# The first and the last expert layer: from sorted tiles to every expert in blocks of 256 tokens

## Chip, cores and metric

One core of one Trainium2 chip. The metric is the device time of one execution in microseconds (us); of several executions the median is taken. The engines are called as in the profile: PE (TensorE, the matrix engine), PEld (its weight loads, which overlap its matmuls), DVE (VectorE), ACT (ScalarE), POOL (GpSimd), SP (SyncE, which only issues DMAs here).

## What is computed

The input is x of 16 sequences of 256 tokens, 128 wide, float32. Three layers act on it, each with a layer norm before it:

```python
x = x + 0.5 * ffn(layernorm(x))        # mixture of experts
x = x + attn(layernorm(x))             # two Mamba blocks, then a linear memory
x = x + 0.5 * ffn(layernorm(x))        # the same mixture again

def ffn(x):                            # E = 8 experts, hidden 512, top 2 of 8
    probs = softmax(x @ gate_w); vals, idx = top_k(probs, 2); vals /= sum(vals)
    combine = zeros(N, E) with vals at idx
    for e in range(E):
        out += combine[:, e:e+1] * (silu(x @ w1s[e]) @ w2s[e])
```

A token needs only its two experts; the other six have a weight of zero.

## The kernel before

The work goes in 8 groups of 2 sequences, that is 512 tokens or 4 tiles of 128 (GROUPS, SEQ, TILES). Each group passes through a first FFN, the mixer (four Mamba passes: two blocks by two sequences, then the memory), and a second FFN. The 16 FFNs of a group of 512 tokens are numbered by `first(g)` and `second(g)` in the order in which they run. The mixer of group g runs in four slots. In each slot the tables of ORDER write out by hand how every engine interleaves the scan's steps with those of an FFN of another group: while the mixer works on group g, the first FFN of g+1 and the second FFN of g-1 are done in pieces (`p` on PE, `F` on ACT, `sc` and `ga` on POOL). So fourteen FFNs lie inside the mixer slots. The first (group 0, number 0) has no mixer before it and is done in `start()`; the last (group 7, number 15) has none after it and is done in `finish()`.

An FFN sorts its tokens by expert. `ffn_stats` and `ffn_norm` (L977) normalise; POOL takes the root (`ffn_root`, L1287) and copies the residual (`ffn_keep`, L1301); `ffn_turn` (L407) transposes on PE, ACT copies (L723), `ffn_gate` (L413) makes the logits, `ffn_top` the two best experts, ACT their weights through a tanh (L728), `ffn_count` (L420 to L424) and `ffn_place` (L1008 to L1031) the place of each of the 1024 token copies in 15 tiles of 128 (NT) that hold one expert each. POOL scatters the copies by 8 indirect DMAs (L1308) to DRAM (`xs_d`, cleared to zero at the start), SP loads them in 5 chunks of 3 tiles (`chunk_in`), and the pieces follow: T transposes a chunk (L432), U multiplies a tile with the first weights of its expert (`ffn_up`, L441, four matmuls of 128x128), ACT applies silu (L747), D multiplies with the second (`ffn_down`, L450, four matmuls). The results go to DRAM by chunks (`chunk_out`), POOL gathers the two rows of each token by 8 indirect DMAs (L1317), and `ffn_sum` (L1048) adds them with their weights to the residual. A float32 matmul is two records in the trace. The first weights of a tile's expert are fetched by SP into a ring of four buffers (`expert_in`, `wst`, 256 KB each), the second ones (`w2s`, 2 MB) lie in SBUF.

`start()` of all engines: FFN 0; halfway through its pieces the routing of FFN 1, whose scatters run beside them; the mixer's constants on DVE (`mixer_weights`, L931 to L960); `ffn_sum` of FFN 0; then the norm, projections and first steps of the mixer of group 0. `finish()` of all engines: DVE closes the last scan (`gate_y`, L1151 to L1157, which waits until the eighth accumulating DMA, L1344, has landed), the memory of sequence 1 runs (`memory_1` to `memory_4`, L579 to L607, with `masked`, L1173, and `mixer_sum`, L1181), and only then the whole of FFN 15, beginning with the norm of all four tiles; the store of group 7 ends the program. Sequence 0 of group 7 has its mixer result in `xb` already in the last slot (`xb` in ORDER).

Of the kernel before, what the change touches and what calls it, by code (L numbers as in the profile page):

```python
# [82 lines left out]
MIDWAY = PIECES // 2  # L83
MIDWAY_LEFT = sum(1 for p in PIECE[:MIDWAY] if p[0] != "D" or p[1] % CH == CH - 1)

# [54 lines left out]
def moe_mamba_kernel(nc, x, pack, early, sel, w1, w2, out):  # L140
# [4 lines left out]
    with ctx:  # L145
# [57 lines left out]
        hit = sb("hit", [P, 2, TILES, E])  # L203
        xa = sb("xa", [P, TILES, D])
# [44 lines left out]
        empty = ys  # L249

# [8 lines left out]
        def sem(name):  # L259
# [19 lines left out]
            sem("f_hmm"), sem("f_hact"), sem("f_ymm"), sem("f_ys"), sem("f_yacc"))  # L279

# [42 lines left out]
        def _(sp):  # L323
# [4 lines left out]
            sp.wait_ge(s_clear, 1)  # L328
# [13 lines left out]
            def chunk_in(n, c):  # L342
                sp.wait_ge(s_scat, 16 * 2 * TILES * (n + 1))
                wait(sp, f_hmm, (n - 1) * ITEMS + RING_OF["T", c] + 1)
                sp.dma_start(xsort[:, c * CH:(c + 1) * CH, :], rows(xs_d[n % 2], c)).then_inc(s_xs[c], 16)

            def expert_in(n, i):
                k = n * NT + i
                sp.wait_ge(f_tile, n + 1)
                if k >= NW:  # L350
                    m, j = divmod(k - NW, NT)
                    sp.wait_ge(f_hmm, m * ITEMS + RING_OF["U", j] + 1)
                e = sp.value_load(eid[n % 2][0:1, i:i + 1], min_val=0, max_val=E - 1)
                sp.dma_start(wst[k % NW][:, :], w1[e]).then_inc(s_w[k % NW], 16)

            def chunk_out(n, c):
                wait(sp, s_gat, 16 * 2 * TILES * (n - 1))
                sp.wait_ge(f_ys, n * CHUNKS + c + 1)
                sp.dma_start(rows(ys_d[n % 2], c), ys[:, c * CH:(c + 1) * CH, :]).then_inc(s_ys[c], 16)
# [6 lines left out]
            def store(g):  # L366
                sp.wait_ge(f_yacc, second(g) + 1)
                sp.dma_start(ot[g], ob[:, :, :]).then_inc(s_store, 16)
# [3 lines left out]
            for n in range(2 * GROUPS):  # L372
# [8 lines left out]
                if n == 0:  # L381
                    for i, b in enumerate(sel_in):
                        sp.dma_start(b, sel[:, i * N_SEL:(i + 1) * N_SEL]).then_inc(s_sel, 16)
                    clear(xs_d[1])
# [8 lines left out]
            store(GROUPS - 1)  # L393
            sp.wait_ge(s_store, 16 * GROUPS)
# [3 lines left out]
        def _(pe):  # L398
# [3 lines left out]
            def ffn_turn(n, busy):  # L402
# [3 lines left out]
                for j in range(TILES):  # L406
# [3 lines left out]
            def ffn_gate(n):  # L410
                pe.wait_ge(f_xT, n + 1)
                for j in range(TILES):
                    last = mm(LG[:, j * E:(j + 1) * E], xT[:, j * P:(j + 1) * P], par("gate"), start=True, stop=True)  # L413
                last.then_inc(f_logits, 1)

            def ffn_count(n):
                pe.wait_ge(f_mask, n + 1)
# [9 lines left out]
            def ffn_sorted(n, c):  # L427
                r = RING_OF["T", c]
                pe.wait_ge(s_xs[c], 16 * (n + 1))
                wait(pe, f_hact, n * ITEMS + r - 1)  # L430
# [4 lines left out]
            def ffn_up(n, i):  # L435
                r, k, t = RING_OF["U", i], n * NT + i, i % CH * P
                pe.wait_ge(s_w[k % NW], 16 * (k // NW + 1))
                wait(pe, f_hact, n * ITEMS + max(r - 1, RING_OF["T", i // CH] + 1))
# [5 lines left out]
            def ffn_down(n, i):  # L444
                pe.wait_ge(f_hact, n * ITEMS + RING_OF["U", i] + 1)
                if i % CH == 0:
                    wait(pe, f_ys, n * CHUNKS + i // CH)
                e = pe.value_load(eid[n % 2][0:1, i:i + 1], min_val=0, max_val=E - 1)
# [9 lines left out]
            def turn(g, i):  # L458
# [4 lines left out]
                if i == 0 and 0 < g < GROUPS - 1:  # L463
                    pe.wait_ge(f_tile, first(g + 1) + 1)
                elif i == 2 and g > 0:
                    pe.wait_ge(f_tile, second(g - 1) + 1)
# [180 lines left out]
            def ffn_pieces(n, a, b):  # L647
                for x in range(a, b):
                    ffn_piece(n, x)

            def route(n):
                ffn_turn(n, None)
                ffn_gate(n)
                ffn_count(n)

            def start():
                route(first(0))
                pe.wait_ge(s_w2, 16)
                ffn_pieces(first(0), 0, MIDWAY)
                pe.wait_ge(f_tile, first(0) + 1)  # L660
                route(first(1))
                ffn_pieces(first(0), MIDWAY, PIECES)
                pe.wait_ge(s_set_dve, 1)
                pe.wait_ge(f_tile, first(1) + 1)
# [6 lines left out]
            def finish():  # L671
                tail = (GROUPS - 1, 1)
                memory_1(*tail, None)
                memory_2(*tail, None)
                memory_3(*tail)
                memory_4(*tail)
                route(second(GROUPS - 1))
                ffn_pieces(second(GROUPS - 1), 0, PIECES)
# [18 lines left out]
        def _(act):  # L697
# [27 lines left out]
            def ffn_gate(n):  # L725
                table(SILUS)
                act.wait_ge(f_gap, n + 1)
                do(th[:, :], gap[:, :], ACT.Tanh, scale=0.5).then_inc(f_th, 1)  # L728

            def ffn_leave(n, x):  # L730
                kind, k = LEAVES[x]
                if kind == "U":
                    table(SILUS)
                if kind == "Y":
                    act.wait_ge(f_ymm, n * NT + (k + 1) * CH)
# [747 lines left out]
```

## Time and profile before

| | us |
|---|---|
| three runs | 1793.55, 1782.19, 1767.53 |
| their median | 1782.19 |
| the profiled execution, its own time | 1785.28 |
| its span, first to last instruction | 1783.4 |
| mean granted TensorE clock in the span | 0.866 of full |

A clock of 1.00 is 2.4 GHz, one of 0.50 is 1.2 GHz; the records know only these two, and a number between is a mean over a stretch. Points of time in the text are us from the start of the span. In the timeline, a row is a run of equal instructions; its bracket gives the idle time of the engine ahead of them and what ended it.

### The profile page before, as it was taken

The numbers are of one execution on the slowest core, as the hardware profiler recorded it, in microseconds if no ns is written. First come the engines' busy times: TensorE is split into PE (matmuls) and PEld (weight loads), VectorE is DVE, ScalarE is ACT, GpSimd is POOL, SyncE is SP. The second block draws the span as 40 slices with busy tenths as digits, with TensorE's granted clock in tenths as the row PEclk, the third lists the DMA queues.
The fourth block names the chain that finished last, engine by engine and source line by source line (L and its number), as shares of the span: only waits on it lengthen the run. The fifth ranks groups of instructions, "written<-read, shape, count | busy, mean of one in ns | idle before, by whom it ended". The sixth has DMA issues, their size and how long they took to land. (4 is left out here: it accounts for less than half of the span.)

```text
span 1783.4 us, 29139 instructions
## 1 busy us (share of the span) xinstructions
PE 1313.4 (74%) x8528; PEld 1183.0 (66%) x8528; DVE 1366.4 (77%) x2144; ACT 1268.3 (71%) x2641; POOL 601.3 (34%) x639
## 2 busy tenths in 40 slices
PE   3738766887888788878888787878888786577434
PEld 2727655776877677767777676767777675567334
DVE  1227798889889888989888888989888979887400
ACT  1229775888789787878789787978787887487212
POOL 2221424144342526152433435163515322321311
PEclk9858967998989899998989899989999898589657
DMA  7415645666576767666666667676666664556323
GB/s 221 135 51 118 133 82 118 140 145 152 128 174 142 168 139 165 137 169 129 138 155 146 158 131 174 138 175 140 154 136 155 142 141 91 112 124 147 63 81 88
DMA packets 153383, 242.49 MB, mean 136 GB/s; under 512 B 14480, under 2 KB 87952, under 8 KB 153104
## 3 DMA queue, kind: packets, MB, share of 16 engines
q0 software_dynamic: 40448, 134.25, 38.9%
q1 hardware_dynamic: 112784, 106.38, 20.7%
q8 instruction: 76, 1.25, 0.3%
q14 instruction: 75, 0.61, 0.1%
HBM read 94.95 MB, written 28.18 MB: 69 GB/s over the span
## 5 line engine op out<-in xcount | busy, mean ns | idle before, releaser
L1344 POOL DMA_DIRECT2D acc<-G x224 | 204.7, 914 | 901.4 <-DVE G L1143 450.8
L809 ACT ACTIVATE dA<-delta,A 128x255 f32<-128x255 f32 x1024 | 425.7, 495 | 4.4 <-DVE hs L1124 3.4
L450 PE MATMUL b_out<-w2s,hT 128*128 x1920 | 282.4, 293 | 66.8 <-issue 44.0
L1130 DVE TENSOR_TENSOR_SCAN hs<-dA,b_r 128x512 f32<-128x512 f32 x256 | 298.9, 1203 | 25.8 <-PE b_r L545 15.2
L1143 DVE TENSOR_TENSOR G<-hs,b_r 128x1024 f32<-128x1024 f32 x224 | 272.3, 1216 | 58.3 <-PE b_r L556 51.3
L450 PEld LDWEIGHTS b_out<-w2s,hT 128*128 128x128 f32 x1920 | 249.6, 202 | 90.2 <-issue 89.0
L1124 DVE TENSOR_TENSOR_SCAN hs<-dA,dbu 128x1024 f32<-128x1024 f32 x128 | 292.6, 2286 | 13.8 <-ACT dA L809 7.3
L441 PE MATMUL b_h<-xsT,wst 128*128 128x128 f32 x1920 | 282.9, 295 | 10.0 <-ACT hT L747 7.3
L441 PEld LDWEIGHTS b_h<-xsT,wst 128*128 128x128 f32 x1920 | 262.3, 211 | 14.7 <-issue 12.2
L705 ACT ACT_TABLE_LOAD x180 | 230.9, 1283 | 4.0 <-PEq L1477 0.7
L825 ACT ACTIVATE scaled<-duT,dtT 128x256 f32<-128x256 f32 x512 | 217.0, 500 | 0.3
L747 ACT ACTIVATE hT<-b_h 128x512 f32<-128x512 f32 x240 | 139.8, 595 | 103.6 <-PE b_h L441 102.3
L545 PE MATMUL b_r<-prm,scaled 128*128 128x128 f32 x1024 | 174.4, 301 | 47.8 <-ACT scaled L825 26.7
L1308 POOL DMA_INDIRECT sorted<-xn,posi x128 | 154.3, 1206 | 105.1 <-DVE posi L1031 70.4
L545 PEld LDWEIGHTS b_r<-prm,scaled 128*128 128x128 f32 x1024 | 135.6, 157 | 61.8 <-issue 27.0
L556 PE MATMUL b_r<-bcr,selr 128*128 128x256 f32 x512 | 137.4, 353 | 48.4 <-DVE G L1143 39.0
L1317 POOL DMA_INDIRECT yk<-results,posi x128 | 139.0, 1086 | 93.5 <-DMA results<-ys 55.3
L1111 DVE TENSOR_TENSOR dbu<-du,b_r 128x1024 f32<-128x1024 f32 x128 | 155.2, 1212 | 12.0 <-PE b_r L538 11.9
L485 PE MATMUL b_w<-uT,inx 128*128 128x256 f32 x512 | 141.6, 414 | 1.4 <-ACT uT L754 1.4
L556 PEld LDWEIGHTS b_r<-bcr,selr 128*128 128x128 f32 x512 | 89.1, 210 | 64.1 <-DVE G L1143 49.4
L485 PEld LDWEIGHTS b_w<-uT,inx 128*128 128x128 f32 x512 | 96.6, 205 | 12.3 <-ACT uT L754 2.3
L432 PE MATMUL b_h<-prm,xsort 128*128 128x128 f32 x240 | 46.2, 307 | 67.2 <-DMA xsort<-sorted 41.6
(155 smaller groups left out, 1788.7 us busy)
## 6 DMA issues: line engine op xcount, KB each, us to landing
acc<-G POOLq DMA_DIRECT2D x224, 512.0 KB
wst<-w_dram SPq DMA_DIRECT2D x240, 256.0 KB, 3.0
xsort<-sorted SPq DMA_DIRECT2D x80, 192.0 KB, 5.6
results<-ys SPq DMA_DIRECT2D x80, 192.0 KB, 3.0
xin<-x_dram SPq DMA_DIRECT2D x8, 256.0 KB, 4.9
sorted<-xn,posi POOLq DMA_INDIRECT x128
yk<-results,posi POOLq DMA_INDIRECT x128
out_dram<-ob SPq DMA_DIRECT2D x8, 256.0 KB, 2.9
```

What stands on the lines that cost most here:

```text
L441: last = mm(H[r % 2][:, w], wst[k % NW][:, w], xsT[i // CH % 2][:, t:t + P], start=True, stop=True)
L450: last = mm(Y[:, i % CH * D:(i % CH + 1) * D], hT[i % NH][:, c, :], w2s[:, e, c, :], start=c == 0, stop=c == HC - 1)
L485: last = mm(o, inx[:, m, r, ch], uT[:, b, PAD - r:PAD - r + T], start=r == 0, stop=r == PAD)
L545: last = nc.tensor.transpose(R[u % 2][:, h * T + t * P:h * T + (t + 1) * P], scaled[k % 2][:, d, t, h * P:(h + 1) * P], ident)
L556: last = mm(C[:, d * T:(d + 1) * T], selr[:, SELECTED.index(DS + DP * j + d), :], bcr[b][:, :], start=True, stop=True)
L705: nc.scalar.preload_act_table_set(name)
L809: last = do(dA[j % 4][:, d, k, 1:], delta[b][:, k, 1:], ACT.Exp, scale=A[:, k, s:s + 1])
L825: last = do(scaled[n % 2][:, d, t, :], duT[b][:, t, :], ACT.Identity, scale=dtT[b][:, s:s + 1])
L1124: V.tensor_tensor_scan(flat(hs[j % 2]), flat(dA[j % 4]), flat(dbu[n % 2]), 0.0, ALU.mult, ALU.add)\
L1130: V.tensor_tensor_scan(hs[j % 2][:, d, :, :].rearrange("p h t -> p (h t)"), dA[j % 4][:, d, :, :].rearrange("p h t -> p (h t)"), R[u % 2][ ...
L1143: V.tensor_tensor(to[:, :, :, :], hs[j % 2][:, :, :, :], both(C).unsqueeze(2).broadcast_to([P, DP, HALVES, T]), ALU.mult).then_inc(q_G, 1)
L1344: Q.dma_start(acc[b][:, :, :, :].rearrange("p d h t -> p (d h t)"), G[j % NG][:, :, :, :].rearrange("p d h t -> p (d h t)"), accum_op=ALU. ...
```

## The change

FFN 0 and FFN 15 don't sort any more. Each is done as 16 blocks: one expert on 256 tokens (two tiles), all eight experts for all tokens. `STARTS` = 16 blocks make FFN 0, in the order expert by expert, both halves of the tokens for each; 16 more make FFN 15, all experts for sequence 0 and then all for sequence 1. FFN 15 is split in two numbers (LAST = 15 and 16), each with its own norm, routing and output store.

A block is `whole_up` (four matmuls with 256 moving columns, `w1` chunks as the stationary operand, the transposed tokens `xTd` moving, into the two banks H), two silus of 128x512 on ACT into `hTd`, `whole_down` (eight matmuls of 128x128 into the one bank OUT) and `whole_sum` on DVE: two scalar_tensor_tensor, which add OUT times the expert's combine weight (`comb`, zero where the expert isn't chosen) to the residual. PE issues `whole_up` of block x+1 ahead of `whole_down` of block x. The wait on `d_sum` keeps `whole_down` of block x behind `whole_sum` of block x-1.

In `start()` the norm, routing, count and placing of FFN 1 are put between these blocks (after blocks 0, 1, 4, 6, 9, 10), and `mixer_weights` after block 10 on DVE. The DMAs of SP are in a new order: the first weights of expert 0 in place of the first clearing of `xs_d`; the other first weights, the second group's x, the constants and then the two clearings behind. In `finish()` the first half (sequence 0) starts ahead of `gate_y`; the memory of sequence 1 lies between its blocks (after 16 to 19), and norm and routing of the second half after blocks 19 to 22. The fourteen sorted FFNs in the slots keep their work; their counters are shifted by one (`m = n - 1`).

```diff
@@ SP
-            clear(xs_d[0])
+            whole_in(0)
             sp.dma_start(w2s ...
-            sp.dma_start(win[:, 0:3 * DI], early[:, 0:3 * DI]).then_inc(s_early, 16)
-            sp.dma_start(taps, early[:, 3 * DI:]).then_inc(s_early, 16)
+            for b in range(2, 2 * NW, 2):
+                whole_in(b)
...
+            load_x(1)
+            sp.dma_start(win[:, 0:3 * DI], early[:, 0:3 * DI]).then_inc(s_early, 16)
+            sp.dma_start(taps, early[:, 3 * DI:]).then_inc(s_early, 16)
+            whole_in(2 * NW)
...
+            clear(xs_d[0])
+            clear(xs_d[1])
+            whole_in(2 * NW + 6)
-            for n in range(2 * GROUPS):
+            for n in range(1, LAST):
...
-            store(GROUPS - 1)
-            sp.wait_ge(s_store, 16 * GROUPS)
+            for b in range(STARTS, STARTS + NW):
+                whole_in(b)
+            store(GROUPS - 2)
+            for b in range(STARTS + NW, STARTS + 2 * E):
+                whole_in(b)
+            for half in range(2):
+                tiles = slice(half * HALF, (half + 1) * HALF)
+                sp.wait_ge(d_sum, STARTS + (half + 1) * E)
+                sp.dma_start(ot[GROUPS - 1][:, tiles, :], ob[:, tiles, :]).then_inc(s_store, 16)
@@ PE
+            def whole_up(x):
+                k = whole_stage(x)
+                pe.wait_ge(s_w[k % NW], 16 * (k // NW + 1))
...
+                half = slice(whole_half(x) * T, (whole_half(x) + 1) * T)
+                for h in range(2):
+                    wait(pe, d_act, 2 * (x - 1) + h + 1)
+                    for c in range(2):
+                        w = slice((2 * h + c) * P, (2 * h + c + 1) * P)
+                        last = mm(H[h][:, c * T:(c + 1) * T], wst[k % NW][:, w], xTd[:, half], start=True, stop=True)
+                    last.then_inc(d_up, 1)
+
+            def whole_down(x):
+                pe.wait_ge(d_act, 2 * x + 2)
+                wait(pe, d_sum, x)
...
+                for j in range(HALF):
+                    for c in range(HC):
+                        last = mm(OUT[:, j * D:(j + 1) * D], hTd(x)[:, c, j * P:(j + 1) * P],
+                                  w2s[:, whole_expert(x), c, :], start=c == 0, stop=c == HC - 1)
+                last.then_inc(d_y, 1)
@@ PE start()
+                for x in range(STARTS):
+                    if x + 1 < STARTS:
+                        whole_up(x + 1)
+                    whole_down(x)
+                    if x == 4:
+                        pe.wait_ge(f_lread, 1)
+                        ffn_turn(first(1), None)
+                    elif x == 6:
+                        ffn_gate(first(1))
+                    elif x == 9:
+                        ffn_count(first(1))
@@ ACT
+            def whole_silu(x):
+                table(SILUS)
...
+                for h in range(2):
+                    act.wait_ge(d_up, 2 * x + h + 1)
+                    wait(act, d_y, x - 1)
+                    do(hTd(x)[:, 2 * h:2 * h + 2, :], both(H[h]), ACT.Silu).then_inc(d_act, 1)
@@ DVE
+            def whole_sum(f, x):
+                dve.wait_ge(f_keep, f[0] + 1)
+                wait(dve, d_sum, x)
+                dve.wait_ge(d_y, x + 1)
+                e = whole_expert(x)
+                for k, j in enumerate(whole_tiles(x)):
+                    last = V.scalar_tensor_tensor(
+                        out=f[2][:, j, :], in0=OUT[:, k * D:(k + 1) * D], scalar=comb[:, j, e:e + 1],
+                        in1=f[2][:, j, :], op0=ALU.mult, op1=ALU.add)
+                last.then_inc(d_sum, 1)
@@ DVE start()
-                route(f)
...
+                whole_weights(f)
+                for x in range(STARTS):
+                    whole_sum(f, x)
+                    if x == 0:
+                        ffn_stats(nx)
+                    elif x == 1:
+                        ffn_norm(nx)
+                    elif x == 6:
+                        ffn_logits(nx)
+                        sorted_top(nx)
+                    elif x == 9:
+                        ffn_place(nx)
+                    elif x == 10:
+                        ffn_weights(nx)
+                        mixer_weights()
@@ DVE finish()
+                ffn_stats(f, one)
+                ffn_norm(f, one)
+                ffn_logits(f, one)
+                ffn_top(f, one)
+                whole_weights(f, one)
                 gate_y(GROUPS - 1, 3)
-                masked(GROUPS - 1, 1)
-                mixer_sum(GROUPS - 1, 1)
...
+                for x in range(STARTS, STARTS + E):
+                    whole_sum(f, x)
+                    if x == STARTS + 1:
+                        masked(GROUPS - 1, 1)
+                    elif x == STARTS + 3:
+                        mixer_sum(GROUPS - 1, 1)
+                        ffn_stats(nx, two)
...
@@ POOL start()
-                for x in range(2 * TILES):
-                    ffn_scatter(f[0], x)
...
-                for x in range(2 * TILES):
-                    ffn_gather(f[0], x)
@@ POOL finish()
-                for x in range(2 * TILES):
-                    ffn_scatter(f[0], x)
-                for x in range(2 * TILES):
-                    ffn_gather(f[0], x)
```

Of the parts left out, `whole_in(b)` fetches the first weights of block b's expert into the ring and waits (`d_up`) until the expert four places earlier has been used; `whole_silu(16)` is issued on ACT ahead of the tanh that makes the first half's weights.

## Rows read from the trace of the kernel before

**Rows 1.** The page, busy time and share of the span by engine

```profile
PE 1313.4 (74%) x8528; PEld 1183.0 (66%) x8528; DVE 1366.4 (77%) x2144; ACT 1268.3 (71%) x2641; POOL 601.3 (34%) x639
```

**Rows 2.** The windows view of the first and the last stages, busy time of each engine

```profile
10.00:38.00 28.00, 7.42 (x31) 6.49 (x31) 4.05 (x32) 2.51 (x4) 8.01 (x8) 1.00 0.62 186
38.00:62.00 24.00, 19.53 (x138) 18.57 (x138) 4.32 (x30) 7.02 (x14) 1.24 (x2) 0.99 0.69 212
62.00:78.00 16.00, 15.39 (x110) 15.20 (x110) 7.84 (x30) 4.98 (x10) 9.37 (x8) 0.80 0.42 124
78.00:98.00 20.00, 4.52 (x36) 3.96 (x35) 2.23 (x14) 1.75 (x4) 7.66 (x8) 0.68 0.55 148
...
1674.00:1690.00 16.00, 9.10 (x34) 7.26 (x34) 4.42 (x14) 1.24 (x3) 0.75 (x2) 0.61 0.00 0
1690.00:1726.00 36.00, 6.57 (x28) 5.98 (x28) 5.16 (x35) 2.08 (x3) 9.06 (x10) 0.50 0.21 62
1726.00:1764.00 38.00, 33.78 (x255) 31.92 (x255) 0.00 (x0) 13.54 (x25) 0.00 (x0) 0.90 0.42 113
1764.00:1784.00 20.00, 0.00 (x0) 0.00 (x0) 2.28 (x8) 0.00 (x0) 7.68 (x8) 0.52 0.17 50
```

**Rows 3.** The timeline around the first FFN: start, duration, engine, line, tiles, idle time

```profile
11.92 1.87 PE L413 MATMUL b_w<-prm,xT 128*128 128x8 f32 x8 [0.69 <-ACT xT L723]
...
36.66 0.87 PE L432 MATMUL b_h<-prm,xsort 128*128 128x128 f32 x3 [16.91 <-DMA xsort<-sorted]
...
72.11 0.36 DVE L931 TENSOR_SCALAR inz<-scaled,prm 128x256 f32<-128x256 f32 x1
...
80.41 0.06 DVE L960 MEMSET gap<- 128x4 f32 x1
...
98.46 2.35 DVE L1048 SCALAR_TENSOR_TENSOR xa<-yk,c,xa 128x128 f32<-128x128 f32 x8 [17.99 <-DMA yk<-results,posi]
...
107.47 1.09 PE L468 MATMUL b_w<-prm,un 128*128 128x128 f32 x4 [23.73 <-DVE un L1079]
...
114.93 1.03 PE L491 MATMUL b_w<-uT,inz 128*128 128x256 f32 x4
```

**Rows 4.** The windows view of PE alone, in stretches of 2 us

```profile
58.00:60.00 2.00, 0.00 (x0) 1.00 0.00 0
60.00:62.00 2.00, 1.69 (x13) 0.86 0.00 0
...
66.00:68.00 2.00, 2.00 (x11) 0.50 0.54 162
68.00:70.00 2.00, 2.00 (x19) 0.94 0.54 168
```

**Rows 5.** The timeline from the last accumulation to the last store

```profile
1669.36 0.90 POOL L1344 DMA_DIRECT2D acc<-G  x1 [4.22 <-DMA acc<-G]
...
1676.39 2.07 PE L579 MATMUL b_w<-yg,prm 128*128 128x256 f32 x4 [12.25 <-DVE yg L1157]
...
1681.56 0.56 DVE L1173 TENSOR_TENSOR SM<-b_w,prm 128x384 f32<-128x384 f32 x1 [5.23 <-PE b_w L593]
...
1687.30 0.42 DVE L1181 TENSOR_TENSOR xb<-b_w,rs 128x256 f32<-128x256 f32 x1 [5.18 <-PE b_w L607]
...
1707.93 0.43 SPq L368 DMA_DIRECT2D out_dram<-ob  x1
...
1712.06 1.11 POOL L1308 DMA_INDIRECT sorted<-xn,posi  x1 [0.20 <-issue]
...
1726.01 0.90 PE L432 MATMUL b_h<-prm,xsort 128*128 128x128 f32 x3 [24.67 <-DMA xsort<-sorted]
...
1742.22 1.06 PE L441 MATMUL b_h<-xsT,wst 128*128 128x128 f32 x8
...
1778.26 2.35 DVE L1048 SCALAR_TENSOR_TENSOR ob<-yk,c,ob 128x128 f32<-128x128 f32 x8 [74.25 <-DMA yk<-results,posi]
1780.64 0.38 SPq L368 DMA_DIRECT2D out_dram<-ob  x1
```

More of the change, by code:

```diff
@@ L82, with whole_stage, whole_expert, whole_half @@
 LEAVES = list(leaves())
-MIDWAY = PIECES // 2
-MIDWAY_LEFT = sum(1 for p in PIECE[:MIDWAY] if p[0] != "D" or p[1] % CH == CH - 1)
+SORTED = 2 * GROUPS - 2
+HALF = T // P
+STARTS = 2 * E
+LAST = 2 * GROUPS - 1
+def whole_stage(x):
+    return x // 2 if x < STARTS else E + SORTED * NT + x - STARTS
+def whole_expert(x):
+    return x // 2 if x < STARTS else x % E
+def whole_half(x):
+    return x % 2 if x < STARTS else (x - STARTS) // E
+def whole_tiles(x):
+    return range(whole_half(x) * HALF, (whole_half(x) + 1) * HALF)
 ORDER = {
@@ L203, in moe_mamba_kernel @@
         hit = sb("hit", [P, 2, TILES, E])
+        comb = sb("comb", [P, TILES, E])
         xa = sb("xa", [P, TILES, D])
@@ L400, in _, with ffn_turn @@
             ident = par("ident")
-            def ffn_turn(n, busy):
+            def ffn_turn(n, busy, tiles=range(TILES)):
                 pe.wait_ge(f_xn, n + 1)
@@ L672, in finish @@
                 tail = (GROUPS - 1, 1)
[L673 to L678, printed above, removed]
+                ffn_turn(LAST, None, range(HALF))
+                ffn_gate(LAST, xTd, range(HALF))
+                whole_up(STARTS)
+                for x in range(STARTS, STARTS + E):
+                    if x + 1 < STARTS + E:
+                        whole_up(x + 1)
+                    whole_down(x)
+                    if x == STARTS:
+                        memory_1(*tail, None)
+                    elif x == STARTS + 1:
+                        pe.wait_ge(f_lread, LAST + 1)
+                        memory_2(*tail, None)
+                    elif x == STARTS + 2:
+                        memory_3(*tail)
+                    elif x == STARTS + 3:
+                        memory_4(*tail)
+                    elif x == STARTS + 5:
+                        ffn_turn(LAST + 1, None, range(HALF, TILES))
+                    elif x == STARTS + 6:
+                        ffn_gate(LAST + 1, xTd, range(HALF, TILES))
+                whole_up(STARTS + E)
+                for x in range(STARTS + E, STARTS + 2 * E):
+                    if x + 1 < STARTS + 2 * E:
+                        whole_up(x + 1)
+                    whole_down(x)
             pe.wait_ge(s_pack, 16)
@@ L886, in finish @@
                 tail = (GROUPS - 1, 1)
[L887 to L891 removed]
+                whole_turned(LAST, slice(0, HALF))
+                whole_silu(STARTS)
+                ffn_gate(LAST, slice(0, HALF))
+                for x in range(STARTS + 1, STARTS + 2 * E):
+                    whole_silu(x)
+                    if x == STARTS + 1:
+                        memory_out(*tail)
+                    elif x == STARTS + 2:
+                        memory_v(*tail)
+                    elif x == STARTS + 3:
+                        memory_reads(*tail)
+                    elif x == STARTS + 6:
+                        whole_turned(LAST + 1, slice(HALF, TILES))
+                    elif x == STARTS + E:
+                        ffn_gate(LAST + 1, slice(HALF, TILES))
             def run(g, n1, n2, n3, is_last):
@@ L974, in ffn_norm @@
                 wait(dve, f_xnT, n)
-                wait(dve, s_scat, 16 * 2 * TILES * n)
-                for j in range(TILES):
+                wait(dve, s_scat, 16 * 2 * TILES * (min(n, LAST) - 1))
+                for j in tiles:
                     last = V.tensor_scalar(xn[:, j, :], src[:, j, :], mv[:, j, 0:1], rstd[:, j:j + 1],
```

304 lines of the change are left out of this document (175 added, 129 removed).

## The prediction

> **What bounds the kernel now.** I began with the page. PE, ACT and DVE are each busy for 71 to 77% of the span and POOL for 34% [rows 1]: no engine is the bound of the whole, and a mean says nothing of one stage. The windows view splits it. The change leaves the fourteen sorted FFNs inside the mixer slots as they are, so only the two ends count.
>
> At the beginning PE is busy for 7.4 of the 28 us from 10 to 38, and for 4.5 of the 20 from 78 to 98 [rows 2]. The timeline says why. The logits of FFN 0 end at 11.92 + 1.87 = 13.8 and PE's first piece begins at 36.66: in between lie count, placing, eight scatters on POOL and the reload. After the last piece come the store, eight gathers, and `ffn_sum`, which ends at 98.46 + 2.35 = 100.8; only then the mixer's norm can begin, and PE goes on at 107.47 [rows 3]. So FFN 0 costs 100.8 - 13.8 = 87.0 us after its logits.
>
> At the end, PE is busy for 6.6 us of the 36 from 1690 to 1726 and for nothing from 1764 to 1784 [rows 2]. The last accumulating DMA is issued by 1669.36 + 0.90 = 1670.3; the memory runs alone on a slow PE from 1676.39; FFN 15 can start at 1687.30 + 0.42 = 1687.7. Its scatters wait for the store of group 6, issued at 1707.93, begin at 1712.06; the first piece is at 1726.01; the last sum starts at 1778.26 and the last store is issued at 1780.64 [rows 5]. The span ends at 1783.4, so the store costs 2.8 us. Both ends are chains of latency (sort, DRAM, gather). The pieces themselves fill 38 us, 1726 to 1764.
>
> **The pace of a block.** Price per record at the full clock: eight 128-column records take 1.06 us [rows 5], and PE passes from one such set to the next at 20 records in 2 us or a little more (the stretch from 68) [rows 4]; I take 0.112 us for one. Four records of 256 columns take 1.03 us [rows 3]. A record's duration has a tail that the next one overlaps: 1.06 - 8 x 0.112 = 0.16. The same tail off 1.03 leaves 0.217 for each. A block is 4 matmuls of 256 columns (8 records) and 8 of 128 (16 records): 8 x 0.217 + 16 x 0.112 = 1.74 + 1.79 = 3.53 us. Sixteen are 56.4 us. For comparison, the sorted layer's 120 matmuls and 15 transposes filled those 38 us with 33.8 busy [rows 2]: the change adds about 22 us of PE work to each end, and takes the latencies away.
>
> Who else could pace a block? ACT has two silus, 0.6 us each by the sorted pieces' (13.5 us busy in 25 instructions from 1726 to 1764, mean 0.54, [rows 2]): 1.2 of 3.53. DVE has two scalar_tensor_tensor of 128x128: eight of them from SBUF take 2.35 [rows 5], so 0.6 for two. Here one operand is in PSUM, which this trace doesn't show for the operation. The nearest rows are 0.42 us for 128x256 and 0.56 for 128x384 with a PSUM source [rows 5]: for two halves between 0.6 and 0.85; I take 0.7, 0.8 with the hand-over. While DVE adds block x-1, PE works on `whole_up(x+1)`, 1.74 us, so the single bank OUT costs nothing as long as DVE has under about 1 us of other work at that point. If that cover were gone entirely, a block would be 0.8 longer, 13 us for each end.
>
> **FFN 0.** It begins with `whole_up(0)` where the count began, 13.8. The second weights are now ahead of the clearing; the first `down` needs them only after two slow `up`, at about 20. The weights of later experts have blocks of 7 us per expert to land. So nothing waits for a DMA; I allow 0 to 3 us.
> - 16 blocks: 56.4 us. FFN 1's transposes (4 records), logits (8) and count (16) on PE are 28 x 0.112 = 3.1.
> - The clock. After a pause PE works at half clock at first. The windows from 1726 to 1764 have a mean clock of 0.90 [rows 2]: 38 x 0.10 x 2 = 7.6 us at half, which then rises and stays. From 60 on, after a pause of over 2 us, it's at half until 68 [rows 4], 0.80 over 16 us being 6.4 us [rows 2]. Work under way for 7 us at half clock costs 3.5 us. The start pays it once.
> - DVE's constants. `mixer_weights` goes from 72.11 to 80.47, 8.4 us [rows 3]. It stands after sum 10. From the end of `down(10)`, PE has `up(12)`, `down(11)`, `up(13)`: 1.74 + 1.79 + 1.74 = 5.3 us. Sum 11 is through after 0.8 + 0.3 (weights) + 8.4 + 0.8 = 10.3. So PE stands for 5.0 us, and such a pause lets the clock fall again [rows 4]: 3.5 more, 8.5 together; bounds 5.0 and 9. The other insertions on DVE (norm, top two, placing) are 1 to 3 us each, and PE has matching work of its own at these points, so nothing.
> - Last sum: 0.8.
> 13.8 + 56.4 + 3.1 + 3.5 + 8.5 + 0.8 = 86.1 against 100.8: **14.7 us gained**. Block 9 ends at 13.8 + 3.5 + 1.7 + 10 x 3.53 + 1.3 = 55.6, count and placing take 4.5 more; FFN 1's eight scatters then run from about 60 to 70, beside the blocks, and its tiles are back well before the mixer's first slot, which needs them 26 us after the sum, as before; the clearings are issued after block 5 and have some 15 us to land before the scatters. The norm of the mixer follows the sum as it did.
>
> **FFN 15.** DVE could take sequence 0's statistics at 1668, but POOL's root stands behind the last accumulating DMA on its queue, 1670.3. Root 1.3, norm of two tiles 0.6, transposes 0.65, copy 0.45, logits at half clock 1.0: `whole_up(16)` starts at 1674.4.
> - 16 blocks 56.4. The memory is 6 records of 256 and 28 of 128 columns: 6 x 0.217 + 28 x 0.112 = 4.4. The second half's transposes and logits, 6 records: 0.7. Cold start 3.3.
> - `gate_y` moves. It stood at 1674; DVE now holds it until the tanh of half one, which on ACT is behind `whole_silu(16)`: 1674.4 + 3.5 (up at half clock) + 0.9 + 1.1 (weights) = 1679.9, plus 2.4 gives 1682.3. `memory_1` is placed behind `down(16)`, which ends at 1674.4 + 5.3 + 3.3 = 1683.0. The wait is hidden by 0.7 us; at worst it costs 2. The other steps of the memory each have a block as cover.
> - Last sum 0.8 and a store of half the size, 2.5.
> 1674.4 + 56.4 + 4.4 + 0.7 + 3.3 + 0.8 + 2.5 = 1742.5 against 1783.4: **40.9 us gained**. Four weight tiles (1 MB) are now fetched at about 1650 beside the last accumulating DMAs, which are on the chain; I give 0.6 for that, bounds 0 and 3.
>
> The sum: 14.7 + 40.9 - 0.6 = 55.0. The profiled execution of 1785.3 becomes 1730.3. The median of the runs lies 3.1 lower, so 1727.2; I say **1729**, between the two.
>
> **A rule that speaks against it.** The granted clock fell only behind pauses: at 60 it dropped to a mean of 0.86 after two microseconds with no matmul, and it was half while PE was busy for the whole of the next stretch [rows 4]; during the sorted pieces of FFN 15, with PE busy for 33.8 of 38 us, it held once up [rows 2]. The blocks wait in each round for a single bank's reader. The Trainium skill, "TensorE: Matmul & The Clock Gate", section "A second HAM failure mode: psum-queue depth-cycling", says that micro-idles between groups of matmuls in such a cycle can make the clock swing between its two levels. This case's sorted pieces, which have short gaps of that kind, show no swing; no row here shows the blocks themselves.
>
> **The rivals.**
> 1. *The clock swings or stays low in the blocks.* For: the clock is 0.866 on average over the span, so it falls often elsewhere, and 0.50 was seen with PE busy all the time (from 66 to 68) [rows 4]. Against: 33.8 of 38 busy without a fall [rows 2]. Half clock throughout would double 56.4 + 56.4 + 8.2, +121 less the 10 already counted, so +111 - 55 = 56 slower, 1785 + 56 = 1841. The gain is gone when half of that is paid: a mean clock of about 0.67 in both stages. Slower than before by over 2% needs a mean below some 0.57. This is the case of the other sign.
> 2. *PE and DVE take turns on the bank OUT.* If a sum takes 2.5 us instead of 0.8 or the hand-overs cost a microsecond, every block is 1 us longer: +32, a gain of 23, 1785 - 23 = 1762, within 2%. For: one bank, a wait in each block. Against: 1.74 us of cover.
> 3. *The weights are late.* Each block pair in FFN 0 and each block in FFN 15 need 256 KB; in FFN 15 that is 256 KB in 3.53 us, 74 GB/s, beside stretches that moved 212 [rows 2]. If every load were 1 us late in the last stage: +16, 1746.
> 4. *More is hidden than I think*: no clock fall at `mixer_weights`, a warm start, 12 us better: 1717.
>
> **Chances.** Forecast with rivals 3 and 4 as its edges 0.84; rival 2, 0.12; rival 1, 0.04, most of it near no change. The runs of before spread from 1767.5 to 1793.6, 13 us to either side, from the slots, which the change doesn't touch. With -12 and +16 of the terms I set 1708 to 1748, and the rivals above this stay outside. A measurement of this kernel can tell about 2% from no change, which is 1746.5: faster 0.84, same 0.13, slower 0.03.
>
> **What would show it.** Right: `whole_sum` of block 15 ends near 86 and the first `un` matmul comes near 93; PE's records come at 3.5 us per block with a granted clock of 1.00, in one stretch from about 20 with a single hole of 5 us after `up(13)`; at the end PE is busy without a hole from 1674 - 15 = 1659 to 1724; no wait on the weights. Wrong: holes ahead of each `down` (rival 2) or ahead of each `up` (rival 3), a clock of 0.50 inside the blocks (rival 1), an `un` matmul not earlier than 100, or slots longer than before by more than the runs' spread, which I have priced at nothing.

## The result and the profile after

The changed kernel takes 1729.5 us (median of 4 runs, 1717.3 to 1734.2) against 1777.2 (median of 4, 1767.5 to 1793.6): ratio 0.970, 95% interval 0.965 to 0.974. That is faster, 0.5 us from the forecast of 1729. The profiled execution has a span of 1715.5 us against 1783.4, so 67.9 less, more than the medians' 47.7. The reading has to say where that comes from.

The page after: PE's share rises from 74 to 78% [rows 1], with more PE work in a shorter span.

```profile
PE 1330.5 (78%) x8754; PEld 1195.6 (70%) x8754; DVE 1379.7 (80%) x2184; ACT 1278.6 (75%) x2657; POOL 568.3 (33%) x610
```

The windows view after, first the four stretches of [rows 2], then the last stage in three (columns as there: stretch, its length, busy of PE, PEld, DVE, ACT, POOL, granted clock, DMA share, GB/s):

```profile
10.00:38.00 28.00, 27.32 (x167) 24.88 (x166) 7.74 (x44) 10.93 (x18) 1.21 (x2) 1.00 0.73 229
38.00:62.00 24.00, 24.00 (x170) 22.74 (x170) 10.56 (x52) 7.26 (x13) 3.62 (x4) 1.00 0.29 81
62.00:78.00 16.00, 11.06 (x54) 9.88 (x54) 7.06 (x29) 2.77 (x5) 6.18 (x5) 0.79 0.14 42
78.00:98.00 20.00, 10.62 (x54) 8.95 (x52) 5.03 (x20) 1.41 (x3) 4.02 (x8) 0.74 0.28 76
1644.00:1660.00 16.00, 15.25 (x76) 13.16 (x77) 5.63 (x26) 6.20 (x11) 0.00 (x0) 0.78 0.25 67
1660.00:1676.00 16.00, 16.00 (x116) 15.20 (x115) 4.02 (x14) 5.16 (x9) 1.27 (x3) 1.00 0.19 57
1676.00:1714.00 38.00, 35.04 (x242) 32.51 (x241) 8.57 (x38) 11.22 (x20) 0.00 (x0) 1.00 0.15 43
```

PE, busy for 7.4 of 28 us from 10 to 38 before, is busy for 27.3. The one hole inside the blocks lies between 62 and 78; behind 83 PE waits for the mixer's norm, as it did before. In the last stage it is busy for 66.3 of the 70 us from 1644 to 1714, where before two stretches of 36 and 20 us held 6.6 us of PE work.

The timeline of the first stage after, to be read against [rows 3]:

```profile
11.06 1.88 PE L471 MATMUL b_w<-prm,yk 128*128 128x8 f32 x8 [0.69 <-ACT yk L838]
12.79 5.42 PE L484 MATMUL b_h<-yk,wst 128*128 128x256 f32 x16
...
61.59 1.89 PE L484 MATMUL b_h<-yk,wst 128*128 128x256 f32 x8
67.67 0.61 DVE L1158 SCALAR_TENSOR_TENSOR xa<-b_out,comb,xa 128x128 f32<-128x128 f32 x2
68.42 3.75 PE L496 MATMUL b_out<-w2s,acc 128*128 128x128 f32 x16 [4.93 <-DVE xa L1158]
71.97 2.97 PE L484 MATMUL b_h<-yk,wst 128*128 128x256 f32 x8
74.77 1.95 PE L496 MATMUL b_out<-w2s,acc 128*128 128x128 f32 x16
81.12 2.02 PE L496 MATMUL b_out<-w2s,acc 128*128 128x128 f32 x16 [0.89 <-DVE xa L1158]
83.28 0.61 DVE L1158 SCALAR_TENSOR_TENSOR xa<-b_out,comb,xa 128x128 f32<-128x128 f32 x2 [2.30 <-PE b_out L496]
90.89 1.08 PE L558 MATMUL b_w<-prm,un 128*128 128x128 f32 x4 [7.74 <-DVE un L1238]
```

L484 is `whole_up`, L496 `whole_down`, L1158 `whole_sum`. The last sum ends at 83.9 in place of 100.8, and the mixer's first transposes come at 90.9 in place of 107.5. The pause of 4.93 us is the one of the constants. The two products behind it take 3.75 and 2.97 us, where the same products take 1.95 and 1.89 otherwise.

The timeline of the last stage after, against [rows 5]:

```profile
1641.49 0.90 POOL L1527 DMA_DIRECT2D acc<-G  x1 [4.23 <-DMA acc<-G]
1646.24 6.09 PE L484 MATMUL b_h<-yk,wst 128*128 128x256 f32 x16
1651.71 0.69 DVE L1310 TENSOR_TENSOR yg<-acc 128x512 f32<-128x512 f32 x1 [0.17 <-issue]
1654.19 1.13 PE L669 MATMUL b_w<-yg,prm 128*128 128x256 f32 x4
1681.06 2.02 PE L496 MATMUL b_out<-w2s,dA 128*128 128x128 f32 x16 [0.54 <-DVE ob L1158]
1710.45 2.02 PE L496 MATMUL b_out<-w2s,dA 128*128 128x128 f32 x16 [0.89 <-DVE ob L1158]
1712.61 0.61 DVE L1158 SCALAR_TENSOR_TENSOR ob<-b_out,comb,ob 128x128 f32<-128x128 f32 x2 [2.30 <-PE b_out L496]
1713.24 0.39 SPq L451 DMA_DIRECT2D out_dram<-ob  x1
```

From the issue of the last accumulating DMA to the end it is 1715.5 - 1642.4 = 73.1 us, before 1783.4 - 1670.3 = 113.1. In neither stage does a row of PE wait for a weight tile.

So in this pair of profiles the two ends give 16.6 (at the mixer's first transposes) and 40.0 us. The remaining 67.9 - 56.6 = 11.3 us lie in the slots between these marks, 1562.8 before and 1551.5 after, which the change doesn't touch.

### The profile page after: what moved, and what is told of

Same layout as the page of the kernel before. It is cut to its first block and busy times, and to the rows that moved or that the text cites. A ratio compares the mean times of both kernels' runs of the same rounds, so it can differ in the third digit from the quotient of the medians.

```text
span 1715.5 us, 29243 instructions
## 1 busy us (share of the span) xinstructions
PE 1330.5 (78%) x8754; PEld 1195.6 (70%) x8754; DVE 1379.7 (80%) x2184; ACT 1278.6 (75%) x2657; POOL 568.3 (33%) x610
## 5 line engine op out<-in xcount | busy, mean ns | idle before, releaser
L540 PE MATMUL b_out<-w2s,hT 128*128 x1680 | 245.7, 292 | 64.9 <-issue 44.2
L540 PEld LDWEIGHTS b_out<-w2s,hT 128*128 128x128 f32 x1680 | 216.2, 201 | 86.3 <-issue 85.3
L528 PE MATMUL b_h<-xsT,wst 128*128 128x128 f32 x1680 | 241.0, 290 | 8.1 <-ACT hT L872 8.1
L528 PEld LDWEIGHTS b_h<-xsT,wst 128*128 128x128 f32 x1680 | 223.9, 207 | 10.6 <-issue 9.9
L646 PE MATMUL b_r<-bcr,selr 128*128 128x256 f32 x512 | 136.3, 350 | 52.2 <-DVE G L1302 40.4
L1488 POOL DMA_INDIRECT sorted<-xn,posi x112 | 137.7, 1229 | 96.5 <-DVE posi L1190 66.8
L872 ACT ACTIVATE hT<-b_h 128x512 f32<-128x512 f32 x210 | 122.0, 595 | 58.7 <-PE b_h L528 57.1
L646 PEld LDWEIGHTS b_r<-bcr,selr 128*128 128x128 f32 x512 | 88.3, 209 | 69.6 <-DVE G L1302 51.0
L1500 POOL DMA_INDIRECT yk<-results,posi x112 | 123.0, 1098 | 35.6 <-issue 33.2
L628 PE MATMUL b_r<-bcr,selr 128*128 128x256 f32 x256 | 67.3, 348 | 38.4 <-DVE hs L1289 38.0
```

Of the source, the lines that this page charges most:

```text
L528: last = mm(H[r % 2][:, w], wst[k % NW][:, w], xsT[i // CH % 2][:, t:t + P], start=True, stop=True)
L540: last = mm(Y[:, i % CH * D:(i % CH + 1) * D], hT[i % NH][:, c, :], w2s[:, e, c, :], start=c == 0, stop=c == HC - 1)
L646: last = mm(C[:, d * T:(d + 1) * T], selr[:, SELECTED.index(DS + DP * j + d), :], bcr[b][:, :], start=True, stop=True)
```

## The experiments

Each experiment starts from the changed kernel, unless it says otherwise. Theory A and its rivals are those of the expectation printed above each result. Three marks in the profiles serve throughout: the end of the last sum of FFN 0 (83.9 in the changed kernel), the slots between the marks above (1551.5), and the time from the result of sequence 0 (`xb` in the last slot) to the end, 1715.5 - 1636.9 = 78.6.

**The changed kernel again.** No edit.

> The changed kernel once more, with nothing edited. The profiled execution of the changed kernel was 68 us shorter than that of before: 16.6 us by the first projection of group 0, 40 us behind the last accumulating DMA, and 11.3 us in the mixer slots between the two (1562.8 us became 1551.5), which the change does not touch. Theory A, the slots vary from run to run by themselves: here the stretch between the two marks lies anywhere from 1550 to 1570 us, the two ends repeat within 1 us (first projection at 91, 73 us behind the last accumulation). Rival B, the shift of the slots' phase makes them shorter: the stretch repeats at 1552 within 3 us. Ratio to before under A 0.968, under B 0.962.

Measured: median 1730.0, ratio 0.9675 (0.965 to 0.970) against 11 runs of before with a median of 1787.7. Span of the profiled execution 1727.3, last sum at 84.2, 73.2 us behind the last accumulation, slots 1562.9. Theory A holds. Over the 14 profiles of this study the slots lie between 1550.5 and 1563.7 us; the lowest is the kernel before with the store moved (below), the next the first execution of the changed one. The 11.3 us of the first pair were a difference between executions, not gain. The gain in the profile is 56.6 us, and the ratio of 0.9675 (58 us of 1787.7) agrees with it.

**Only the first layer in blocks.** The last FFN sorted as before: SP's loop to `range(1, LAST + 1)`, `SORTED = 2 * GROUPS - 1`, and the four `finish()` of before.

> FFN 0 in blocks, FFN 15 sorted as before. Theory A, the two ends' gains are independent: the first projection stays at 91 us as in the changed kernel, and what follows the last accumulating DMA is 113 us again; the median is 16 to 17 us below before (1761), ratio 0.991. Rival B, that an earlier start is given back in the slots: no gain, ratio 1.00.

Measured: median 1766.9, ratio 0.990 (0.986 to 0.993): under 2%, but clear of no change. That is 18 us by the ratio and 21 by the medians (1787.7 less 1766.9). The first transposes stand at 91.9; 113.6 us behind the last accumulation; slots 1554.7. The first stage keeps its gain without the second, so an earlier start isn't given back in the slots; the last stage is worth the other 40 (113.6 against 73.1 in the profiles, 37 between the medians). A kernel with only the last layer in blocks wasn't run.

**The store first, in the kernel before.** SP issues the store of group 6 ahead of the weights of FFN 15; its old place is left out for that FFN.

```diff
+                if n == 2 * GROUPS - 1:
+                    store(GROUPS - 2)
                 for i in range(NW):
                     expert_in(n, i)
-                if n in seconds and n - 1 in seconds:
+                if n in seconds and n - 1 in seconds and n < 2 * GROUPS - 1:
                     store(seconds[n - 1])
```

> The kernel before, in which SP stores group 6 ahead of the weights of FFN 15 instead of behind them. Theory A: 8 of the 40 us of the last stage were this one queue order, since POOL's copy waited for the store until 1711.2 while the places were known at 1703.9: the time behind the last accumulation falls from 113.1 to 105 us, ratio to before 0.9955. Rival B: the scatters find another wait and the gain is under 3 us.

Measured: median 1776.1, ratio 0.995 (0.992 to 0.998), small but clear of no change. Behind the last accumulation it is 105.2 us, 7.9 less. In the kernel with only the first layer in blocks, whose last stage has the old order, POOL's copy waits for the store:

```profile
1684.65 0.43 SPq L409 DMA_DIRECT2D out_dram<-ob  x1
1688.44 0.61 POOL L1436 TENSOR_SCALAR ob<-xb 128x512 f32<-128x512 f32 x1 [21.58 <-DMA out_dram<-ob]
1689.25 1.12 POOL L1443 DMA_INDIRECT sorted<-xn,posi  x1 [0.20 <-issue]
```

with the store ahead, the scatters follow the places directly:

```profile
1700.22 1.11 POOL L1310 DMA_INDIRECT sorted<-xn,posi  x1 [13.37 <-DVE posi L1033]
```

A fifth of the last stage's gain was to be had by one queue order, with no change of the algorithm. The other 32 us came with the blocks.

This profile shows a second thing, in FFN 0, which the edit doesn't touch. Its last sum ends at 108.0 in place of 100.8 and the mixer's first transposes come at 114.7 in place of 107.5. While POOL's eight scatters of FFN 1 run (66.0 to 76.0), ACT waits for something that the profile calls "remote", and PE stands behind it:

```profile
76.76 0.49 ACT L741 ACTIVATE ys<-b_out 128x384 f32<-128x384 f32 x1 [3.07 <-remote]
...
78.23 2.07 PE L452 MATMUL b_out<-w2s,hT 128*128 x8 [4.64 <-ACT hT L749]
```

So the first stage of the kernel before differs by 7 us between two executions, and the gain there is 16.6 us against one of them and 23.8 against the other; the medians, with 18 to 21, lie between.

**Constants in four portions.** `mixer_weights` cut into four: its two norm inputs behind sums 10 and 11, taps and the selection copies behind 12, the rest behind 13.

> The constants of the mixer on DVE in four portions behind the sums of blocks 10 to 13 in place of one of 8.5 us behind block 10. Theory A, my price of 8.5 us for that step (5.0 us in which PE stands and 3.5 us of half clock after it): the last sum of FFN 0 ends at 75.5 us in place of 83.9, ratio to the changed kernel 0.995. Rival B, the clock costs nothing extra: 5 us, 79. Rival C, the work only moves, because PE waits at each portion: 82 to 84.

Measured: median 1723.1, ratio to before 0.964 (0.961 to 0.966), against the changed kernel's 1730.0 on the same chip 6.9 us less. Its profiled execution gained only 2.4 us at the first mark (81.5), which is none of the three forecasts: both DVE and ACT stood still for five microseconds, at a place where nothing in the program holds them. DVE and ACT in that stretch:

```profile
62.52 0.61 DVE L1162 SCALAR_TENSOR_TENSOR xa<-b_out,comb,xa 128x128 f32<-128x128 f32 x2 [0.91 <-PE b_out L496]
...
69.90 0.61 DVE L1162 SCALAR_TENSOR_TENSOR xa<-b_out,comb,xa 128x128 f32<-128x128 f32 x2 [4.91 <-remote]
...
69.86 1.09 ACT L847 ACTIVATE acc<-b_h 128x512 f32<-128x512 f32 x2 [5.11 <-remote]
```

Where the profile says "remote" it names no engine and no DMA of this core as the releaser. By the program DVE's sum waits here for PE's `down` of block 12, whose records end at 65.9, and ACT's silu for the next `up` and for that same `down`. Two more runs took this up.

> The kernel of spread_consts for one more look. Its profiled execution had a stretch of 4.9 us in which DVE and ACT both waited though the product that they wait for had ended, which no edit explains. Theory A, this belongs to that one execution: the last sum of FFN 0 ends at 75.5 us here, without that stretch. Rival B, it comes with this order of the work: the same stretch again, end at 81.5.

Measured: the same stretch, 4.8 us until 69.97, last sum at 79.9. Rival B: it comes again with this order of the work.

> The constants in four portions, and besides, POOL scatters FFN 1's tokens behind the roots of the mixer (from about 85 us) and no longer beside blocks 10 to 12. Both looks at the kernel of spread_consts showed DVE and ACT waiting 4.8 to 5.1 us until 69.9, for a product of PE that the records have ended at 65.8; eight scatters ran from about 58 to 68.5. Theory A, the scatters or their transfers hold it up: without them at that time the stretch is gone and the last sum of FFN 0 ends at 75.5 to 76.5 us. Rival B, it has nothing to do with them: the same stretch, end at 79.5 to 81.5. The later scatters may cost a few us at the start of the slots under either.

Measured: the stretch is gone, DVE's waits are about 1 us and the last sum ends at 77.6, 6.3 to 6.6 us ahead of the changed kernel's; median 1718.9 (1717.4 to 1720.0), ratio 0.961 (0.956 to 0.967).

```profile
63.49 0.61 DVE L1162 SCALAR_TENSOR_TENSOR xa<-b_out,comb,xa 128x128 f32<-128x128 f32 x2 [0.91 <-PE b_out L496]
...
67.01 0.61 DVE L1162 SCALAR_TENSOR_TENSOR xa<-b_out,comb,xa 128x128 f32<-128x128 f32 x2 [1.06 <-PE b_out L496]
...
83.88 1.23 POOL L1498 DMA_INDIRECT sorted<-xn,posi  x1 [0.19 <-issue]
```

With the scatters moved, the stretch is gone (theory A, though the end came 1.1 us behind its range). It was seen only beside scatters, in four profiles: both of this kernel, the combined one below, and the kernel before with the store moved. But scatters alone don't make it: in the other nine profiles with scatters at that place no row shows it; with two banks, for one, ACT works on beside them at 66.5 and 67.4. One more difference is in the rows: in each of those nine one scatter takes 2.0 to 2.4 us, in the four with the stretch none takes over 1.24. By what way scatters and stretch hang together (descriptors, transfers, a late signal of PE, whose ends the profile only models) no run here shows.

The price of my step, 8.5 us, was 6.3 to 6.6 by the end of the last sum. The blocks before came 1.6 us later here than in the first profile of the changed kernel; counted from the start of sum 10 to that of the last sum it is 17.0 us here against 24.9 and 23.6 in the two profiles of the changed kernel, so 7.9 and 6.7.

**Two banks.**

```diff
                 pe.wait_ge(d_act, 2 * x + 2)
-                wait(pe, d_sum, x)
+                wait(pe, d_sum, x - 1)
...
-                        last = mm(OUT[:, j * D:(j + 1) * D], hTd(x)[:, c, j * P:(j + 1) * P],
+                        last = mm((OUT, C)[x % 2][:, j * D:(j + 1) * D], hTd(x)[:, c, j * P:(j + 1) * P],
```

and the same choice in `whole_sum`.

> Every second block's second product goes to another PSUM bank, so that it waits for the sum two blocks back. Theory A, the single bank costs nothing in the steady blocks, because the next block's first product covers the sum: a block stays at 3.51 us; only the pause at the constants shrinks from 4.9 to about 1.4 us, with perhaps no fall of the clock, and the last wait of 0.9 us goes at each end: first sum group ends 4.5 to 8 us earlier, the last stage 1 to 1.5 us shorter. Rival B, PE and DVE take turns on the bank: a block falls below 3.4 us and each end gains 5 us or more in the steady part.

Measured: median 1722.6, ratio 0.964 (0.960 to 0.967), 7.4 us below the changed kernel. The last sum ends at 76.8, 7.1 us earlier, and `xb` to the end is 76.7, 1.9 less. PE and the clock at the constants:

```profile
65.44 1.89 PE L484 MATMUL b_h<-yk,wst 128*128 128x256 f32 x8
68.77 2.02 PE L496 MATMUL b_r<-w2s,acc 128*128 128x128 f32 x16 [1.44 <-ACT acc L847]
70.63 1.89 PE L484 MATMUL b_h<-yk,wst 128*128 128x256 f32 x8
```

```profile
66.00:68.00 2.00, 1.34 (x7) 0.83 (x5) 1.73 (x13) 1.19 (x2) 1.60 (x2) 1.00 0.44 161
68.00:70.00 2.00, 1.23 (x11) 1.26 (x12) 1.22 (x4) 0.00 (x0) 1.44 (x2) 1.00 0.11 33
```

A pause of 1.44 us left the clock at 1.00. In the changed kernel, the same stretches behind a pause of 4.93 read:

```profile
66.00:68.00 2.00, 0.00 (x0) 0.00 (x0) 1.72 (x14) 0.00 (x0) 1.69 (x2) 0.83 0.39 139
68.00:70.00 2.00, 1.58 (x7) 1.61 (x8) 0.28 (x2) 0.00 (x0) 1.10 (x2) 0.50 0.17 51
70.00:72.00 2.00, 2.00 (x12) 2.00 (x11) 0.00 (x0) 0.00 (x0) 0.00 (x0) 0.50 0.08 23
```

A steady block is 3.52 us with two banks (sums at 70.93 and 74.45) and 3.51 with one. That is theory A; the last stage gained 1.9 us where I said 1 to 1.5. How long a pause has to be isn't settled by this: with four portions of constants PE stood for 3.02 us in one profile, and the two products behind took 2.70 and 2.93 us, with a clock of 0.50 from 72 to 74; in the other it stood for 2.93, and they took 2.02 and 1.89 at 1.00.

**A slower sum.** The opposite test of the same cover: four more scalar_tensor_tensor per block, into a spare tile.

> Four more scalar_tensor_tensor per block in DVE's sum, written to a spare tile nobody reads: the sum's two instructions take 0.61 us, six will take 1.66. In the changed kernel the sum starts 0.30 us behind the end of a block's second product, and PE goes on 0.14 us behind the sum's end. Theory A, the next block's first product (1.73 us) covers all of this: only 0.30 + 1.66 + 0.14 - 1.73 = 0.37 us show, a block takes 3.88 in place of 3.51, and the two stages together are 11 to 13 us longer. Rival B, PE and DVE take turns on the bank: the whole 1.05 us show, a block takes 4.56, 32 us in all.

Measured: median 1741.0, 11 us above the changed kernel's 1730.0. The last sum ends at 92.3, 8.1 to 8.4 later, and `xb` to the end is 86.0, 7.4 more. Two blocks:

```profile
26.89 2.02 PE L497 MATMUL b_out<-w2s,acc 128*128 128x128 f32 x16 [0.20 <-DVE xa L1165]
28.75 1.89 PE L485 MATMUL b_h<-yk,wst 128*128 128x256 f32 x8
30.84 2.02 PE L497 MATMUL b_out<-w2s,acc 128*128 128x128 f32 x16 [0.20 <-DVE xa L1165]
```

The starts of the two `down` lie 3.95 us apart: of 1.1 us more on DVE, 0.44 show (I said 0.37). The cover is real and ends where I put it; in the changed kernel DVE has some 0.6 us of it left in each block (1.05 less 0.44).

**The pause filled.** 20 matmuls `mm(C[:, 0:P], ident, ident)` ahead of `whole_down(12)`.

> The changed kernel with 20 more matmuls of 128x128 on PE (their result is read by nobody) where it stands while DVE makes the mixer's constants: about 4.5 us of work in the pause of 4.9 us. The clock fell to 0.50 behind that pause and the next two products took 3.75 and 2.97 us in place of 1.95 and 1.89. Theory A: without the pause in PE's work the clock stays at 1.00, and the last sum of FFN 0 ends at about 80.7 us in place of 83.9, though DVE still takes as long. Rival B, the half clock comes from something else (DMA or DVE load at that time): the end stays at 83 to 84.

```profile
65.27 4.63 PE L476 MATMUL b_r<-prm 128*128 128x128 f32 x40
70.38 2.02 PE L500 MATMUL b_out<-w2s,acc 128*128 128x128 f32 x16 [0.48 <-issue]
72.24 1.89 PE L488 MATMUL b_h<-yk,wst 128*128 128x256 f32 x8
```

Measured: the products behind it run at 2.02 and 1.89 us: the clock stays up, so it is PE's own pause that lets it fall. From the start of sum 11, behind the constants, to that of the last sum it is 82.48 - 69.63 = 12.9 us; without the filling 83.28 - 67.67 = 15.6 in the changed kernel, 14.3 in its second profile and 15.8 with only the first layer in blocks. The clock's share of the pause is 1.4 to 3.0 us, not 3.5. The end at 83.1 isn't 80.7, because in this execution the blocks before came 2 us later (sum 11 at 69.6 in place of 67.7; in the second profile of the changed kernel it is at 69.2). The median, 1729.7, is the changed kernel's 1730.0: too small an effect for the runs.

**Warm starts.** 15 matmuls on the cleared tile `ys` ahead of the first transposes and 34 on the identity ahead of the last FFN's.

> The changed kernel with idle matmuls on PE ahead of both block stages: 15 on a cleared tile from about 2.5 us, 34 on the identity ahead of the last FFN's first transposes. Theory A: both stages begin at full clock; the first two blocks' first products take 3.6 us in place of 5.4 and 6.1, transposes and logits half; last sum of FFN 0 ends 3.3 us earlier, the time from the result of sequence 0 (xb) to the end falls from 78.6 by 3.4. Ratio to the changed kernel 0.996. Rival B: products of zeros don't hold the clock, or the added matmuls delay the real ones: start unchanged or later.

```profile
2.56 5.83 PE L476 MATMUL b_h<-ys 128*128 128x128 f32 x30 [2.56 <-POOL ys L1465]
...
11.64 3.85 PE L488 MATMUL b_h<-yk,wst 128*128 128x256 f32 x16
...
1646.21 3.90 PE L488 MATMUL b_h<-yk,wst 128*128 128x256 f32 x16
```

Measured: median 1724.7, 5.3 below the changed kernel's. The first two products take 3.85 and 3.90 us in place of 5.42 and 6.09; the last sum ends at 79.8, 4.1 earlier; `xb` to the end 75.7, 2.8 less. The first stage was warmed by products of zeros, the last by products of the identity, and 3.85 and 3.90 us show no difference.

**An early root.** `ffn_stats` of sequence 0 ahead of `ffn_sum` of FFN 14, `ffn_root` ahead of the last accumulating DMA.

> DVE takes sequence 0's statistics ahead of the weighted sum of FFN 14, and POOL its root ahead of the last accumulating DMA. Theory A, my step that the last stage's start hangs on POOL's queue behind that DMA (root at 1642.1, DVE idle 2.4 us for it): the last stage starts 2.5 to 3 us earlier, the time from xb to the end falls from 78.6 to about 76. Rival B: what then comes last is the sum of FFN 14, whose buffer the transposed tokens share, or the landing of the last accumulation: 78.

```profile
1650.73 0.23 POOL L1469 TENSOR_TENSOR rstd<-mv,epst 128x2 f32<-128x2 f32 x1 [1.36 <-DVE mv L1051]
...
1653.48 0.68 PE L469 MATMUL b_w<-prm,xn 128*128 128x128 f32 x2 [5.11 <-DVE xn L1111]
1653.62 0.95 POOL L1532 DMA_DIRECT2D acc<-G  x1 [1.85 <-DMA acc<-G]
1655.50 6.09 PE L488 MATMUL b_h<-yk,wst 128*128 128x256 f32 x16
```

Measured: median 1715.6 (7 runs, 1713.5 to 1726.6), ratio 0.960 (0.956 to 0.963). From `xb` (1649.4) the blocks start after 6.1 us, before after 9.3; to the end it is 75.4, 3.2 less. That is theory A. The median fell by 14, more than the mark: its profiled execution is also the slowest of its seven. What the other 11 us are isn't settled; the slots would have to be shorter in the executions that weren't profiled.

**All together.** Four portions, two banks, 15 and 20 idle matmuls, early root.

> The changed kernel with four portions of constants, two banks, 15 idle matmuls ahead of the first blocks and 20 ahead of the last FFN's, and the early statistics and root. If the gains add: the last sum of FFN 0 ends at about 71 us (84 in the changed kernel), the time from sequence 0's result (xb) to the end falls from 78.5 to about 71, the median is 1709, ratio to before 0.957, to the changed kernel 0.988. Rival: DVE's order, with four portions in a row, becomes the bound where PE was, and half of the first stage's gain is lost: 1715.

Measured: median 1708.5 (1703.2 to 1719.9), ratio to before 0.958 (0.954 to 0.961), to the changed kernel 0.988. `xb` to the end is 71.5, and the median is 0.5 us from the 1709 that I said, in part by chance, since one mark isn't met: the last sum ends at 74.9, not 71. Most of that is a mistake in my sum: four portions and two banks remove the same pause, so their gains don't add. Two banks (76.8) and the warm start (4.1) alone would give 72.7. The stretch beside the scatters is there again (DVE 4.91 us, ACT 5.10) and costs PE 1.19; some 1 us stays open. The rival didn't come: the last sum waits for PE, not for DVE's constants. It is the fastest version run; the later scatters weren't put into it.

## Why the prediction was right

The gain that I forecast, 55 us, stands against 56.6 at the two ends in the profiles, 47.7 between the first medians and 57.7 between the second.

**Pace of a block.** 3.53 us forecast, 3.51 measured, with the granted clock at 1.00 from 1660 to 1714 and no hand-over cost. The way to it, taking a record's tail off by a stream of equal records, holds for 256 columns too.

**FFN 0.** 14.7 us forecast, 16.9 measured at the last sum. Three small terms were off. The logits ended at 12.9, not 13.8: the parameters, issued at the same time as before, landed 0.9 us earlier (ACT's first use of them at 6.87, before at 7.74), which I had left at nothing. What follows them in the queue is now first weights and not a clearing; whether that is the reason no run tested. The cold start cost about 1.6 us in the products, not 3.5 (5.42 us against 3.77 for 16 such records in a row at 1682.9): it began with the logits, so part of it was over. The clock behind the pause cost 1.4 to 3.0, not 3.5. Against me, the last block's second product waits 0.9 us, since no first product stands ahead of it. The base was one execution: against the other profile of the old first stage (108.0) the same end is a gain of 24.1. The pause itself, 5.0 forecast, was 4.93.

**FFN 15.** 40.9 forecast, 40.0 measured. From the last accumulation's issue to the first product 4.1 forecast, 3.85 measured; `gate_y` 5.5 us behind that product forecast, 5.47 measured. The cold start cost 2.3 us in the products (6.09 against 3.77), not 3.3. The memory's first step began 0.06 us behind the end of `gate_y`, so the 0.7 us of slack that I had counted on weren't there: PE stood for some 0.2 us. Missed were the two waits at the ends of the halves (0.54 and 0.89), where again no first product covers the sum.

**The slots.** The 0.6 us for the four early weight tiles can't be seen under a spread of 13 us in the profiles. The weak step was to set the total on one profiled execution less 1 to 3 us: the medians of before were 1777 to 1788 in the comparisons. That 1729 was met to 0.5 us is luck; that the gain lies at 48 to 58 us isn't.

**The rivals.** Clock (1): no fall in the blocks, except behind the pause; half clock besides only at the two cold starts. The Trainium skill, "TensorE: Matmul & The Clock Gate", section "A second HAM failure mode: psum-queue depth-cycling", tells of a kernel in bf16 whose clock swings by micro-idles between groups of matmuls. In this float32 kernel, with waits of up to 0.9 us on a bank's reader, and a pause of 1.44 with two banks, the clock stayed at 1.00, so this case doesn't show it. Bank (2): excluded for the steady blocks by two banks and by the slower sum; the single bank costs only at the constants and at the end of each half. Weights (3): no wait in the trace; not tried by an edit. Rival 4's idea, more hidden or warm, needed edits to come true, and then gave 5 to 7 us each in the medians.

## What to carry to other kernels

Where a layer stands alone at an end of the program, count its chain of latencies against the work that it saves: here each end took on about 22 us more of matrix work and still became about 17 to 24 and 40 us shorter, because sorting, DRAM and gathering went. The fourteen layers whose latencies lie beside other work stayed sorted; blocks weren't tried there. Keep the next product ahead of the one that waits for a reader, look for blocks where there is none, and cut long preparations on another engine into portions smaller than that cover. Before a gain is read from one profile, split it at marks, and set aside the stretch that the edit didn't touch.

## What the runs showed that I had not expected

- Beside the eight scatters DVE and ACT waited for 4.8 to 5.1 us in both profiles of one kernel and in the combined one; with the scatters elsewhere it was gone. The sorted first stage has such a stretch too (ACT 3.07 us, PE 4.64) in one of two executions. The way is open.
- The granted clock reads 1.00 from 10 to 38 us in the changed kernel, while its first 16 records of 128x256 take 5.42 us, and 3.85 with PE warmed. At the start of a trace durations tell the clock, the recorded level doesn't.
- Untouched slots differ by 13 us of 1560 between executions, and the untouched first stage of before by 7, in steps that no edit explains.
